# Routing logits from a three-part bfloat16 split at the head of the next turn, and three elementwise steps placed on other engines

## What is computed

```python
h = layernorm(x)                                    # per row
Xw = h @ Wv + bv
e = leaky_relu(sj + si + ab, 0.2)                   # sj, si: Xw against two columns
T = adj * exp(e); T = T / sum(T)                    # 128 x 128 per graph
x1 = x + relu(h@Wk0 + T@h@Wk1 + T@T@h@Wk2 + biases)
xf = layernorm(x1)
logits = xf @ switch_w.T + switch_b                 # 16 experts
route, p = argmax, max of softmax(logits)
pos = place of the row among the rows of its expert; keep = pos < 1228
y = xf @ expert_w[route].T + expert_b[route]
out = x1 + (y if keep else xf) * p
```

## Time and profile before

| | value |
|---|---|
| median of 3 runs | 741.64 us (740.81 to 742.03) |
| the profiled execution | 743.05 us, with a span of 741.3 us |
| PE, busy share of the span | 95% |
| PEld | 84% |
| DVE | 86% |
| ACT | 65% |
| POOL | 62% |
| share of PE in the chain that ended last | 86% |

### The profile page before, as it was taken

One profiled execution on the slowest core, in us unless ns is written; L12 is line 12 of the kernel. 1 busy time (PEld: TensorE's weight loads), 2 busy tenths in 40 slices (PEclk: granted clock), 3 DMA queues, 4 the chain that ended last, 5 costly groups with the idle time before them and its releaser, 6 DMA issues.

```text
span 741.3 us, 17931 instructions
## 1 busy us (share of the span) xinstructions
PE 707.4 (95%) x4714; PEld 620.0 (84%) x4714; DVE 639.5 (86%) x3129; ACT 480.8 (65%) x1509; POOL 456.6 (62%) x542
## 2 busy tenths in 40 slices
PE   8999999999999999999999999999999999968784
PEld 7888788788998998888989989889888888857673
DVE  6899999999998999999999989999999998867462
ACT  3567677667666667676676766676767667654451
POOL 6446666546666676666666666766666666565554
PEclk9999999999999999999999999999999999987997
DMA  9976565534443454444354334444443322254430
GB/s 283 206 181 159 158 167 155 145 117 149 130 131 124 155 158 152 151 151 148 127 156 139 120 122 154 155 140 152 143 131 135 109 102 90 86 175 144 117 108 6
DMA packets 95458, 104.33 MB, mean 141 GB/s; under 512 B 10729, under 2 KB 85622, under 8 KB 95360
## 3 DMA queue, kind: packets, MB, share of 16 engines
q1 hardware_dynamic: 77104, 65.97, 30.1%
q0 software_dynamic: 15376, 34.30, 14.7%
q10 hardware_dynamic: 2880, 2.92, 1.6%
HBM read 54.13 MB, written 54.76 MB: 147 GB/s over the span
## 4 chain that ended last, share of the span: by engine, by line
PE 86%; DVE 6%; issue 3%; ACT 1%; DMA 1%; POOL 1%; another core or an unknown queue 0%; SPq 0%; POOLq 0%; DVEq 0%; ACTq 0%
PE ps_z12a L1359 11%; PE ps_z12b L1359 11%; PE ps_lgb L1359 9%; PE ps_z0a L1359 8%; PE ps_z0b L1359 7%; PE ps_lga L1474 6%; PE ps_z0a L1442 4%; PE ps_z0b L1442 4%; PE ps_z12b L1421 4%; PE ps_xt L1461 4%; PE ps_xt L1389 3%; PE ps_lgb L1505 3%; PE ps_z12a L1421 3%; PE ps_t L1435 2%; PE ps_t L1410 2%
## 5 line engine op out<-in xcount | busy, mean ns | idle before, releaser
L587 POOL DMA_INDIRECT out<-lent,tok x143 | 145.6, 1018 | 156.2 <-DVE lent L1273 134.7
L574 POOL DMA_INDIRECT rowbuf<-rows,idx x128 | 130.3, 1018 | 52.4 <-issue 27.4
L652 ACT CAST xth<-ps_xt 128x256 fp32r<-128x256 f32 x128 | 47.9, 374 | 95.7 <-PE ps_xt L1389 94.8
L519 POOL TENSOR_SCALAR x<-xin,nm,r 128x256 f32<-128x256 f32 x128 | 84.5, 662 | 16.5 <-PE ps_xt L1389 10.5
L726 ACT ACTIVATE x<-rin 128x255 f32<-128x255 f32 x143 | 86.8, 608 | 3.1 <-DMA rin<-rowbuf 2.4
L1474 PEld LDWEIGHTS ps_lga<-swc,xft 128*128 128x128 f32 x512 | 76.5, 190 | 10.8
L707 ACT ACTIVATE od<-rows,oc,oa 128x256 f32<-128x256 f32 x128 | 77.0, 602 | 0.1
L1474 PE MATMUL ps_lga<-swc,xft 128*128 128x16 f32 x512 | 65.7, 242 | 0.0
L948 DVE TENSOR_TENSOR em<-e 128x128 f32<-128x128 f32 x128 | 40.1, 314 | 26.1 <-ACT e L674 25.1
L868 DVE TENSOR_TENSOR xtl<-ps_xt,xth 128x256 fp32r<-128x256 f32 x128 | 53.9, 421 | 9.4 <-ACT xft L699 7.6
L673 ACT ACTIVATE e<-ps_t,svs 128x128 f32<-128x128 f32 x128 | 47.1, 368 | 22.7 <-PE ps_t L1435 20.6
(11 more groups left out here) (223 smaller groups left out, 2363.1 us busy)
## 6 DMA issues: line engine op xcount, KB each, us to landing
rin<-rowbuf SPq DMA_DIRECT2D x143, 130.0 KB
out<-od SPq DMA_DIRECT2D x32, 512.0 KB
xin<-in_x SPq DMA_DIRECT2D x31, 512.0 KB, 4.4
ain<-in_adj SPq DMA_DIRECT2D x32, 256.0 KB, 4.6
ewr<-in_ewT SPq DMA_DIRECT2D x16, 256.0 KB, 3.9
ewr<-negs POOLq DMA_DIRECT2D x16, 256.0 KB, 5.1
out<-lent,tok POOLq DMA_INDIRECT x143
rowbuf<-rin ACTq DMA_DIRECT2D x1, 2080.0 KB, 20.1
```

The lines of the kernel that those rows point to most:

```text
L519: pool.tensor_scalar(x0[:, g % 2, :], xin[:, g % BODY, :], nm1[:, q, g % G:g % G + 1], r1[:, q, g % G:g % G + 1], ALU.add, ALU.mult).then_ ...
L574: pool.indirect_dma_start(out=rowbuf, out_offset=bass.IndirectOffsetOnAxis(ap=idx[:, i:i + 1], axis=0), in_=rows[:, r, :], in_offset=None, ...
L587: pool.indirect_dma_start(out=out.rearrange("g n d -> (g n) d"), out_offset=bass.IndirectOffsetOnAxis(ap=tok[:, i % RY:i % RY + 1], axis=0 ...
```

## The change

The logits are no longer two float32 matmuls. The turned rows are split exactly into three bfloat16 parts and so are the switch weights, and six bfloat16 matmuls of 128x48 (three parts of the rows, two halves of the features, against the three parts of the weights side by side) fill three sums per expert, which DVE adds up every fourth turn. ACT rounds the rows to bfloat16 as the first part while it copies them (`xft`), DVE subtracts it from the float32 rows (`xfr`, a new instruction of 128x256 a turn), whose upper halves are the second part, and POOL subtracts these (`xf3`, new). The logits of graph k-3 move from late in turn k to the head of turn k+1. POOL no longer normalises the graphs' rows (but for the first four): it makes `nr1` every fourth turn, and ACT makes `x0` with one instruction, where `od` was; `od` moves to the end of ACT's turn. The weights' split (`switch_parts`) runs once.

```diff
@@ POOL slot_fn
                     elif g % G == 0:
                         pool.wait_ge(s_ve1, bat(it, g) + 1)
+                        ge(pool, s_x0, it * BODY + g - G)
                         pool.tensor_tensor(r1[:, q, :], ve1[:, q, :], mhalf[:], ALU.pow).then_inc(s_r1, 1)
                         pool.wait_ge(s_r1, bat(it, g) + 1)
-                    ge(pool, s_x0t, it * BODY + g - 1)
-                    alone(pool)
-                    pool.tensor_scalar(x0[:, g % 2, :], xin[:, g % BODY, :], nm1[:, q, g % G:g % G + 1],
-                                       r1[:, q, g % G:g % G + 1], ALU.add, ALU.mult).then_inc(s_x0, 1)
+                        pool.tensor_tensor(nr1[:, q, :], nm1[:, q, :], r1[:, q, :], ALU.mult).then_inc(s_nr1, 1)
...
+                if valid(it, k - LAG_XFT):
+                    last_part(it, k - LAG_XFT)
...
+            def last_part(it, g):
+                pool.wait_ge(s_xfr, it * BODY + g + 1)
+                pool.tensor_tensor(xf3[:], xfr[:], upper(xfr[:]), ALU.subtract).then_inc(s_xf3, 1)
@@ POOL, after the turns
+            last_part(IT, BODY - 2)
             for g in range(OUT_LEFT - IT * BODY, G30):
                 row_scatter(IT, g)
+            last_part(IT, BODY - 1)
             tokens(IT, G30)
@@ ACT slot_fn
-                go = k - LAG_OUT
-                if valid(it, go):
-                    default_rows(it, go)
+                gn = k + LEAD_X0
+                if valid(it, gn) and it * BODY + gn >= G:
+                    normalised(it, gn)
...
                     norm(i)
+                go = k - LAG_OUT
+                if valid(it, go):
+                    default_rows(it, go)
@@ DVE slot_fn, right behind xtl
+                if valid(it, k - LAG_XFT):
+                    middle_part(it, k - LAG_XFT)
...
+            def middle_part(it, g):
+                dve.wait_ge(s_xfe, it * BODY + g + 1)
+                ge(dve, s_xf3, it * BODY + g)
+                dve.tensor_tensor(xfr[:], ps_xt[:, D:2 * D], xft[:], ALU.subtract).then_inc(s_xfr, 1)
@@ DVE scaled_logits
                 dve.wait_ge(s_log, b + 1)
+                dve.tensor_reduce(lgs[:], log_span(g // G % 2, 0, G).rearrange("p (g c e) -> p g e c", c=3, e=E),
+                                  AX_X, ALU.add).then_inc(s_lgs, 1)
                 dve.wait_ge(s_r2, b + 1)
-                dve.tensor_tensor(lg[:], per_expert(ps_log[:, g // G % 2 * G * E:(g // G % 2 + 1) * G * E]),
-                                  over_experts(rows[:, r:r + G, RSTD]), ALU.mult).then_inc(s_lgr, 1)
+                dve.wait_ge(s_lgs, b + 1)
+                dve.tensor_tensor(lg[:], lgs[:], over_experts(rows[:, r:r + G, RSTD]), ALU.mult).then_inc(s_lgr, 1)
@@ PE slot_fn
                 if valid(it, gx - 1):
-                    pe.wait_ge(s_xfe, n(gx - 1))
+                    logits(it, gx - 1)
...
-                if valid(it, gx):
+                if it * BODY + k == B:
                     logits(it, gx)
@@ PE logits
-                pe.wait_ge(s_xfe, it * BODY + g + 1)
+                pe.wait_ge(s_xf3, it * BODY + g + 1)
...
-                for t in range(KT):
-                    mm = pe.matmul(ps_log[:, (b2 * G + j) * E:(b2 * G + j + 1) * E], xft[:, t * P:(t + 1) * P],
-                                   swc[:, t, :], start=(t == 0), stop=(t == KT - 1), skip_group_check=True)
+                parts_of = [xft[:], upper(xfr[:]), xf3[:]]
+                for n, part in enumerate(parts_of):
+                    for t in range(KT):
+                        mm = pe.matmul(log_span(b2, j), part[:, t * P:(t + 1) * P],
+                                       swp[:, t].rearrange("p c e -> p (c e)"), start=(n == 0 and t == 0),
+                                       stop=(n == 2 and t == KT - 1), skip_group_check=True)
```

More of the change, by code:

```diff
@@ L156, in graph_then_experts @@
         swc = sb("swc", [P, KT, E])
-        xft = sb("xft", [P, D])
+        swp = sb("swp", [P, KT, 3, E], BF16)
+        swr = sb("swr", [P, 2, KT, E])
+        xft = sb("xft", [P, D], BF16)
+        xfr = sb("xfr", [P, D])
+        xf3 = sb("xf3", [P, D], BF16)
+        lgs = sb("lgs", [P, G, E])
         lg = sb("lg", [P, G, E])
@@ L270, in graph_then_experts @@
         s_xfe = sem("s_xfe")
+        s_xfr = sem("s_xfr")
+        s_xf3 = sem("s_xf3")
+        s_swp = sem("s_swp")
+        s_lgs = sem("s_lgs")
         s_log = sem("s_log")
@@ L323, in bat, with upper, log_span @@
             return it * NB + rel // G
+        def upper(v):
+            return v.bitcast(BF16).rearrange("p (d h) -> p d h", h=2)[:, :, 1]
+        def log_span(b2, j, m=1):
+            o = (b2 * G + j) * 3 * E
+            return ps_log[:, o:o + m * 3 * E]
+        SWS = slice(2 * G * 3 * E, 2 * G * 3 * E + E)
         def xr(i):
@@ L551, in slot_fn, with switch_parts @@
                                    accum_op=ALU.add).then_inc(d_ewd[e % EPP], 16)
+            def switch_parts():
+                pool.wait_ge(s_swc, 1)
+                pool.tensor_copy(swp[:, :, 0, :], swc[:]).then_inc(s_swp, 1)
+                pool.wait_ge(s_swp, 1)
+                pool.tensor_tensor(swr[:, 0], swc[:], swp[:, :, 0, :], ALU.subtract).then_inc(s_swp, 1)
+                pool.wait_ge(s_swp, 2)
+                pool.tensor_copy(swp[:, :, 1, :], swr[:, 0]).then_inc(s_swp, 1)
+                pool.wait_ge(s_swp, 3)
+                pool.tensor_tensor(swp[:, :, 2, :], swr[:, 0], swp[:, :, 1, :], ALU.subtract).then_inc(s_swp, 1)
+            def last_part(it, g):
+                pool.wait_ge(s_xfr, it * BODY + g + 1)
+                pool.tensor_tensor(xf3[:], xfr[:], upper(xfr[:]), ALU.subtract).then_inc(s_xf3, 1)
             def row_factors(it, g):
@@ L696, in slot_fn, with normalised @@
                     norm(i)
+                go = k - LAG_OUT
+                if valid(it, go):
+                    default_rows(it, go)
+            def normalised(it, g):
+                q = g // G % 2
+                j = slice(g % G, g % G + 1)
+                if g % G == 0:
+                    act.wait_ge(s_nr1, bat(it, g))
+                if it * BODY + g == G:
+                    act.wait_ge(s_x0, G)
+                act.wait_ge(s_x0t, it * BODY + g - 1)
+                act.activation(x0[:, g % 2, :], xin[:, g % BODY, :], ACT.Identity, bias=nr1[:, q, j],
+                               scale=r1[:, q, j]).then_inc(s_x0, 1)
             def turned_rows(it, g):
@@ L1447, in slot_fn @@
                     for t in range(KT):
-                        mm = pe.matmul(ps_log[:, 2 * G * E:2 * G * E + E], onesf[:], sw[:, t, :],
+                        mm = pe.matmul(ps_log[:, SWS], onesf[:], sw[:, t, :],
                                        start=(t == 0), stop=(t == KT - 1))
```

19 lines of the change are left out of this document (15 added, 4 removed).

## The result

The changed kernel takes 786.02 us (median of 4 runs, 784.91 to 786.61) where the kernel before takes 741.72 on the same chip (740.81 to 742.03). The ratio is 1.0598, 95% interval 1.0579 to 1.0616: slower, by 44 us. The forecast was 778 with a range of 752 to 796, so its side and its range held, and the time came out 8 us longer. As the experiments show, the nearness is partly luck: two edits were costed at nothing, of which one gives 7.7 us and the other costs some 13 more than was reckoned for it.

The account below looks back on a forecast made before the run. PE bounds the kernel, but DVE's added 1.72 us per four turns meets 1.73 spare in woven turns (1.14 early), so DVE joins the bound. Woven 22.1, early 9.1 and tail 5.1 make 36.3 on 743.05: 778 us, range 752 to 796.

Parts of the forecast that it names:

- the path: Hops between engines through four woven turns, `xtl` to `xtl`: 21.29 us against 20.37, +0.92, over 24 groups +22.1.
- Early turns: Turns without a tile, DVE splitting expert weights: +0.58 to +1.72 us per four, taken as +1.3; seven groups, +9.1.
- PE's gain: Six bfloat16 logits matmuls at 0.25 us replace 0.35 of float32: 0.10 us a turn, from 0.22 to a loss of 0.18.
- A: Woven turn where DVE names rows: `xtl` to `svs` 1.27 us, then 3.71 by way of PE to the next `xtl`.
- C: Woven turn that scales logits: `xtl` to `svs` 1.47 us, then 2.07 by PE to the next head.
- B: Second of four woven turns: `xtl` to `svs` 1.17 us, then 4.43 by DVE's own queue to the next `xtl`.
- D: Woven turn where PE counts: head to the transpose of `svs` 3.32 us, 1.51 to `em`, 2.34 to the next `xtl`.
- Edits costed at nothing: ACT's `x0` with `od` moved, and POOL's last part at 0.7 to 0.8 us, both fit in idle time: no cost.
- The tail: Behind the last turn, POOL's last part waits for `xfr` ahead of `tokens`, delaying the last logits: +5.1 us (0 to 6).
- PE stays the bound: Rival: DVE's waits swallow all its new work and PE's gain remains, -12 us: 730 to 736; chance 0.08.
- DVE's filled waits: Rival: DVE fills its waits but for the small gaps, woven group 20.85 us: 762 us; chance 0.17.
- the head becomes dearer: Rival: six logits matmuls at 0.53 us add 0.28 at each of three heads, +20: 798 us; chance 0.17.

Follow-up runs that it names:

- no_last_part: Changed kernel without POOL's last part (second part multiplied twice in its place): 770.26 us, ratio 1.0349.
- no_parts: Changed kernel without both remainders, DVE's `xfr` and POOL's last part (the logits take the first part three times): 748.71 us, ratio 1.0065.
- tile_split_first: Changed kernel with DVE's split of the woven tile (`xtl`) ahead of the next input's statistics instead of behind them: 790.14 us, ratio 1.063.
- dve_load_alone: Kernel before with only DVE's subtraction (128x256) added behind `xtl`, its result not used: 759.36 us, ratio 1.0197.
- x0_on_act: Kernel before with only the exchange: ACT makes `x0` where `od` stood, `od` ends its turn, POOL makes `nr1`: 736.64 us, ratio 0.9887.
- parts_on_pool: Changed kernel with DVE's subtraction gone: ACT copies the rows in float32 and POOL makes both remainders: 784.95 us, ratio 1.054.

## Why the prediction was right, and where it was not

- **What bounds.** Right. DVE had 1.73 us to spare in four woven turns, and the change brought it past that; the loss is 43.2 us up to the last logits. DVE's share of the chain went from 6% to 35%, though DVE is not full: it is idle 1.39 us of 21.50.
- **The subtraction.** `xfr` at 0.41 us a piece as forecast; by itself 15.0 us where the path gives 20 with the logits in their old place; beside the other edits 21 (no_last_part against no_parts, (1.0349 - 1.0065) x 744). Early turns were oversized: 5.9 by itself and 6.4 in all, not 9.1.
- **PE's gain.** Oversized as a cost: six matmuls take 0.17 us of the chain, not 0.25, strided weights included. The 0.49 us that the prediction holds against it was worked out with a figure for matmuls of 128 columns; these have 48, so it did not bear on them. That the gain bought nothing, since PE waits elsewhere, is read from the waits and was not run by itself.
- **The path.** Each hop came within 0.54 us and the sum within 0.22. But the sum is near because this group is a short one: on average four woven turns went from 20.47 to 21.74, +1.27 where the forecast had +0.92, which is the 8 us that the woven part came out longer (30.3 for 22.1). The hops from `svs` to the next head by way of PE were longer (in A 340.29 to 342.51, which is 2.22; in C 2.29; forecast 2.07), and they hold a step that failed: "less the 0.35 of the moved logits this is 2.07". Taking the logits out from between the tile's split and its products does not return 0.35 us; the products wait for the split instead. By itself the move costs 5.8 us. From B's head to `xtl` it was 1.79 for 1.64, with `xth` 0.20 late in between. Against these, D's transpose to `em` was 0.54 shorter. One term was also added up short: "the sum and the multiplication behind it, some 0.50" is 0.36 + 0.26 = 0.62 by the prediction's own rows (269.05, 269.31).
- **"Edits costed at nothing", ACT's `x0`.** Wrong, in sign: the exchange gives 7.7 us. The cover was there on ACT. What was not looked at is what `x0` on POOL might cost DVE; the rows of `em`, `rows` and `svs` speak for it, that of `tm` against it, and the cause of the gain stays argued.
- **"Edits costed at nothing", POOL's last part.** Wrong for the turns: the part is worth 18.5 us, of which some 5 lie in the tail, where its place had been forecast, and some 13 were put at nothing. Its 0.62 us and its time against the next head were right, for PE waits for it 3.6 us in all, in the last two turns only. In the woven turns the traces show 7.4 us. With the part, two things come late there: `svs` in B, by 0.23 us, because DVE's `full` ahead of it is longer beside the part (5.6 us over the woven turns; it is also why B's `xtl` to `svs` is 1.39 for 1.17), and `xth`, just behind POOL's scatters. Which of them makes the 7.4 us was not tried; that it is the lateness of `xth` alone is unlikely, for in tile_split_first that grows by 21 us and the woven part by 3.9.
- **The tail.** +6.6 for +5.1, by the mechanism described.

By ratio to before, the runs that take the change apart step by step add up: without both remainders +4.8, with the subtraction +21.1 more, with the last part +18.5 more, together 44.5 us. The edits run alone give less: exchange -7.7, logits' place +5.8, subtraction +15.0, and with the last part 31.6. Of the remaining 13 some 6 are what the subtraction costs more beside the other edits than alone. The other 7 lie in no_parts: the sum over three parts, the six matmuls in place of the float32 ones, and how these act with the exchange and the logits' place. They were not run by themselves; by the forecast's 0.36 us in 31 groups the sum could hold all of them. The rivals: that PE stays the bound falls with the result and with dve_load_alone, and so does the 762 of DVE's filled waits; that the head becomes dearer by its matmuls falls with their 0.17 us. (In the filled waits' sum the 0.49 of small gaps is 0.54 by its rows, 1.73 less 0.88 and 0.31.)

## What to carry to other kernels

A matmul that seems movable may be the cover of another engine's work: before moving it, look at which signal the next instruction behind it waits for, and how much earlier that signal would have to come. An instruction moved from DVE to POOL is not free on DVE: here a two-input instruction of DVE went from 225 to 613 ns on average. Compare the mean duration of DVE's instructions, all of them, with and without it. When a queue is retimed by a new wait, price what is behind that wait too: POOL's last part made PE wait in the last two turns only, where it was looked for, and cost some 13 us where it was not.

## What the runs showed of the hardware

- Where ACT's `xth` was due shortly after the second scatter of POOL's pair (1.0 to 1.4 us behind its start), it came late in all 38 such woven turns of the changed kernel, mostly 0.6 us after the scatter's end; over 1.6 us behind the start it was not late. What holds it up stays open: behind a single scatter it was late in 19 of 20 such turns of no_parts, 0.3 us after the end, and in none of 9 of x0_on_act.
- DVE's two-input instruction of 64 elements took 0.99 us beside a two-input instruction of POOL in parts_on_pool, and 613 ns on average there; 225 ns in the changed kernel.
- DVE's one-input instruction of 16 elements (`full`) held its queue for 0.30 us on average where POOL's last part ran beside it (24 woven turns of the changed kernel), and for 0.07 without the part (no_last_part).
- bfloat16 matmuls of 128x48 in a row take 0.028 us each in the chain (0.17 for six), also with weights read at a stride of two elements.
